# Window attention, MLP and an inverted bottleneck on one core: depthwise matrices placed by the host and scaled on GpSimd, the attention bias looked up by rows, x loaded per group

## The chip, the core and the metric
One core of a Trainium2 chip. The metric is the device time of one execution in microseconds (us). TensorE (PE), VectorE (DVE), ScalarE (ACT), GpSimd (POOL) and SyncE (SP, which here only issues DMAs) each run a program of their own in order and meet at semaphores. All data are float32.

## What is computed
x is (4, 48, 128, 128). The first layer is a Swin block without shift, the second an inverted residual with batch norms:

```python
h = layernorm(x) cut into 8x8 windows of 64 tokens, 48 channels, 4 heads of 12
attn = softmax(q @ k.T * scale + rpb_table[rel_idx])       # bias (64, 64) a head, the same in every window
x = x + proj(attn @ v)
x = x + fc2(gelu(fc1(layernorm(x))))                       # 48 -> 192 -> 48
h = relu(bn1(w1 @ x))                                      # 48 -> 288
h = relu(bnd(depthwise3x3(h, wd)))                         # 288 channels
out = x + bn2(w2 @ h)                                      # 288 -> 48
```

## The kernel before
Three stages follow each other, each a pipeline written out by hand with a loop in its middle.

**Attention** (`attention`, from L232) works on 128 groups of 4 pairs of windows, 512 tokens each. Step i of every engine handles different stages of groups i-3 to i+4. DVE sums and centres group i+4 (L509, L528), GpSimd squares and scales (L624, L615), TensorE turns it and makes queries and keys of group i+2 (L449, L469), ACT copies the keys out (L595), and SyncE moves them by four DMAs into `kb`, the right operand of the scores (L410). The first 64 rows of `kb` hold the bias, the first 64 rows of `qa` an identity, so the score product L441 adds the bias itself. All of x lies in one tile `scratch`. ACT loads its first groups (L356), SyncE the rest in three DMAs (L400), in its program ahead of the keys' DMAs.

Before the first step, `prepare_tables` (L81) does two things in the same tile `scratch`. It looks the bias up: the indices of all 4096 pairs are spread to 128 partitions, cast, compared with the partition's number (L161, L164), and the one-hot matrix is multiplied with the table, 512 columns at a time (L211); the result, 4 x 4096, goes to DRAM and from there, spread, into `kb` (L137, L143). And it builds the depthwise matrices: a 3x3 filter over a patch of 10x10 inputs and 8x8 outputs is a matrix of 100 rows and 64 columns for each of 288 channels. 192 products of the scaled taps with a tensor of places (L222) make them, DVE and ACT copy them out (L185, L201), and SyncE stores them to `conv_mats` in DRAM, nine parts of 32 channels (L148). Row 100 of each carries the batch norm's shift. The x loads of L400 wait for these stores.

**MLP** (`mlp`, L630) works on 64 strips, 5.8 us each, and writes the image rows to `img_mid` in DRAM.

**Convolution** (`conv`, L805) has its GpSimd program written before that of `mlp`, and those of SyncE, TensorE, ACT and DVE behind it; each engine runs its programs in the order in which they are written. There are 8 half images and 3 chunks of 96 channels in each, so k = 0 to 23. A half image is cut on GpSimd into patches `xp`: 16 pieces, each two DMAs into one of five slots and a copy (L930). The first half is loaded by GpSimd itself, piece by piece (L985), as soon as its image is stored; later ones by SyncE (L1020). Its GpSimd order at the start is: constants (L964), weight loads (L973), the clearing of `yc` (L974, L976), the 16 pieces, the borders. DVE folds the batch norms into the weights (L1172 to L1191) after its MLP program. Chunk k on TensorE is the depthwise stage (L1084, three thirds with a tile `mats` each), then the products of w2 (L1118) mixed with the first products of chunk k+1 (L1066). SyncE asks for the next matrices third by third as the depthwise stage lets go of them (L1028), in the first chunk of a half followed by the pieces of the next half. TensorE's first product waits for the cut of the first half (`border_set`) and for the weights.

Of the kernel before, what the change touches and what calls it, by code (L numbers as in the profile page):

```python
# [28 lines left out]
P = 128  # L29
# [29 lines left out]
TAPROW = 32  # L59
# [21 lines left out]
def prepare_tables(nc, d, block, scratch, psum, kb, kb_set):  # L81


# [7 lines left out]
    taps = sb("taps", [P, HID1])  # L91
    gd, vd, md, bd = (sb(n, [TAPROW + 1, HID1]) for n in ("gd", "vd", "md", "bd"))
    sd, shift = sb("sd", [TAPROW + 1, HID1]), sb("shift", [TAPROW + 1, HID1])
    eps = sb("eps_d", [P, 1])


    size = [POUT * P, CH * POUT]
    scratch = scratch[:, scratch.shape[1] - size[0] - 2 * size[1]:]
    places = scratch[:, 0:size[0]].rearrange("q (o i) -> q o i", o=POUT)
    onehot = scratch[:, size[0]:size[0] + 2 * NT * NT].rearrange("q (t n) -> q t n", t=2)  # L100
    idsf = scratch[:, size[0] + 2 * NT * NT:size[0] + 3 * NT * NT]
    bias = idsf[0:NH, :]
    mats = [scratch[:, size[0] + size[1] * k:size[0] + size[1] * (k + 1)].rearrange("q (c o) -> q c o", o=POUT)
            for k in range(2)]
    cleared, loaded, ids_loaded, cast = sem("t_cleared"), sem("t_loaded"), sem("ids_loaded"), sem("ids_cast")
    hot, looked_up, copied, stored, kb_loaded = (
        sem(n) for n in ("hot", "looked_up", "b_copied", "b_stored", "kb_loaded"))
    bn_loaded, table_loaded = sem("bn_loaded"), sem("table_loaded")
    root, scaled = sem("d_root"), sem("d_scaled")
    mat_ready, copied_v, copied_a = sem("mat_ready"), sem("mat_cv"), sem("mat_ca")  # L110
    mats_stored = [sem(f"mat_stored{k}") for k in range(2)]
    K = TAPROW + 1
    UNIT = 4
    NU = POUT // UNIT
    BLOCKS = NT * NT // 512

    @block.gpsimd
    def _(pool):
        for n, (t, value) in enumerate(((eps[:, :], EPS), (table[:, :, :], 0.0), (taps[:, :], 0.0),
                                       (places, 0.0))):  # L120
            nc.gpsimd.memset(t, value).then_inc(cleared, 1)
            pool.wait_ge(cleared, n + 1)

    @block.sync
    def _(sp):
        for dst, src in ((ids[:, :], d["rel_idx"].partition_broadcast(P)), (number[:, :], d["number"])):
            sp.dma_start(dst, src).then_inc(ids_loaded, 16)
        for t, n in ((vd, "vd"), (gd, "gd"), (md, "md"), (bd, "bd")):
            sp.dma_start(t[:, :], d[n].partition_broadcast(K)).then_inc(bn_loaded, 16)
        sp.wait_ge(cleared, 2)  # L130
        for t, rows in ((0, slice(0, P)), (1, slice(P, d["table"].shape[0]))):
            sp.dma_start(table[0:rows.stop - rows.start, t, :], d["table"][rows, :]).then_inc(table_loaded, 16)
        sp.wait_ge(cleared, 4)
        sp.dma_start(taps[0:9, :], d["wd"]).then_inc(loaded, 16)
        sp.dma_start(places[0:K, :, :], d["places"]).then_inc(loaded, 16)
        sp.wait_ge(copied, BLOCKS)
        sp.dma_start(d["rel_bias"], bias).then_inc(stored, 16)  # L137
        sp.wait_ge(stored, 16)
        sp.wait_ge(*kb_set)
        for s in range(2):  # L140
            for h in range(NH):
                src = d["rel_bias"][h].rearrange("(n m) -> n m", m=NT)
                sp.dma_start(kb[s][0:NT, :, h, :], bc(src, 1, 2 * PAIRS)).then_inc(kb_loaded, 16)  # L143
        for c in range(CHUNKS):
            sp.wait_ge(copied_v, NU // 2 * (c + 1))
            sp.wait_ge(copied_a, NU // 2 * (c + 1))
            for u in range(LOADS):
                sp.dma_start(d["conv_mats"][LOADS * c + u], mats[c % 2][0:MROWS, TCH * u:TCH * u + TCH, :])\  # L148
                    .then_inc(mats_stored[c % 2], 16)

    def mats_free(eng, c):

        if c == 1:
            eng.wait_ge(stored, 16)
        if c >= 2:
            eng.wait_ge(mats_stored[c % 2], 16 * LOADS * (c // 2))

    @block.vector
    def _(dve):
# [3 lines left out]
        for t in range(2):  # L163
            nc.vector.tensor_scalar(onehot[:, t, :], idsf, number[:, t:t + 1], None, ALU.is_equal).then_inc(hot, 1)  # L164
        dve.wait_ge(root, 1)
        nc.vector.reciprocal(vd[:, :], sd[:, :]).then_inc(scaled, 1)
        dve.wait_ge(scaled, 1)
        nc.vector.tensor_tensor(sd[:, :], vd[:, :], gd[:, :], ALU.mult).then_inc(scaled, 1)
        dve.wait_ge(scaled, 2)
        nc.vector.tensor_tensor(md[:, :], md[:, :], sd[:, :], ALU.mult).then_inc(scaled, 1)  # L170
        dve.wait_ge(loaded, 32)
        nc.vector.tensor_tensor(taps[0:9, :], taps[0:9, :], sd[0:9, :], ALU.mult).then_inc(scaled, 1)
        dve.wait_ge(scaled, 4)
        nc.vector.tensor_tensor(shift[:, :], bd[:, :], md[:, :], ALU.subtract).then_inc(scaled, 1)
        dve.wait_ge(scaled, 5)
        nc.vector.tensor_copy(taps[TAPROW:K, :], shift[0:1, :]).then_inc(scaled, 1)
        for j in range(0, BLOCKS, 2):
            dve.wait_ge(looked_up, j + 1)
            nc.vector.tensor_copy(bias[:, 512 * j:512 * j + 512], psum[0:NH, j, :]).then_inc(copied, 1)
        for c in range(CHUNKS):  # L180
            mats_free(dve, c)
            for u in range(NU * c, NU * (c + 1), 2):
                dve.wait_ge(mat_ready, u + 1)
                j = UNIT * (u % NU)
                nc.vector.tensor_copy(mats[c % 2][0:MROWS, :, j:j + UNIT].rearrange("q c o -> q o c"),  # L185
                                      psum[0:MROWS, u % 8, 0:UNIT * CH].rearrange("q (o c) -> q o c", c=CH)).then_inc(copied_v, 1)

    @block.scalar
    def _(act):
        act.wait_ge(bn_loaded, 64)  # L190
        act.wait_ge(cleared, 1)
        nc.scalar.activation(sd[:, :], vd[:, :], ACT.Sqrt, bias=eps[0:K, :]).then_inc(root, 1)
        for j in range(1, BLOCKS, 2):
            act.wait_ge(looked_up, j + 1)
            nc.scalar.activation(bias[:, 512 * j:512 * j + 512], psum[0:NH, j, :], ACT.Copy).then_inc(copied, 1)
        for c in range(CHUNKS):
            mats_free(act, c)
            for u in range(NU * c + 1, NU * (c + 1), 2):
                act.wait_ge(mat_ready, u + 1)
                j = UNIT * (u % NU)  # L200
# [5 lines left out]
    def _(pe):  # L206
# [10 lines left out]
        for u in range(CHUNKS * NU):  # L217
            if u >= 8:
                pe.wait_ge(copied_a if u % 2 else copied_v, (u - 8) // 2 + 1)
# [1087 lines left out]
```

## Time and profile before

| what | value |
|---|---|
| median of 3 runs | 2379.42 us (2370.36 to 2392.66) |
| the profiled execution, its own time | 2378.27 us |
| its span | 2376.5 us |
| PE busy | 2216.1 us (93%) |
| PEld (weight loads, beside PE) | 1575.1 us (66%) |
| DVE busy | 1560.4 us (66%) |
| ACT busy | 1392.0 us (59%) |
| POOL busy | 408.3 us (17%) |
| mean granted TensorE clock | 0.975 |

The span runs from the first to the last instruction of the profile. "Idle before" in a row is the time its engine stood still ahead of it, and the arrow names what ended that. A float32 product appears as two records of TensorE. SPq, ACTq and the DMA lines of POOL are the issuing of DMAs, not their transfers.

### The profile page before, as it was taken

How to read it: one execution, taken by the hardware profiler on the slowest of the kernel's cores; microseconds unless marked ns; L12 is line 12 of the kernel's file. 1: busy time of each engine (PE TensorE's matmuls, PEld its weight loads, DVE VectorE, ACT ScalarE, POOL GpSimd, SP SyncE). 2: the span in 40 equal slices, each digit the busy share in tenths (PEclk: the TensorE clock that was granted, in tenths of full speed). 3: DMA queues.
4: the chain of work that ended last, by engine and by line, in shares of the span. 5: the costliest groups of instructions: out<-in, count | busy, mean ns of one | idle time of the engine just before them, and what ended most of it. 6: DMA issues, size and time to landing. Idle time of an engine off the chain costs nothing.

```text
span 2376.5 us, 71361 instructions
## 1 busy us (share of the span) xinstructions
PE 2216.1 (93%) x27044; PEld 1575.1 (66%) x27044; DVE 1560.4 (66%) x2869; ACT 1392.0 (59%) x2896; POOL 408.3 (17%) x796
## 2 busy tenths in 40 slices
PE   5499999999999995999999899999999999989997
PEld 3477777777777774333333577767777776767774
DVE  5279999999999896333333566657565666656663
ACT  1367777777777773555555455556556565555653
POOL 2023333333333334513000010101010101001000
PEclk9799999999999997999999999999999999999999
DMA  3811111111111111545444433526172535343411
GB/s 121 310 41 51 54 51 54 51 54 51 54 51 54 51 55 56 129 119 139 117 113 114 112 79 91 114 68 138 49 149 56 113 93 106 89 99 69 117 52 28
DMA packets 272936, 208.57 MB, mean 88 GB/s; under 512 B 228011, under 2 KB 261401, under 8 KB 262217
## 3 DMA queue, kind: packets, MB, share of 16 engines
q1 hardware_dynamic: 269992, 200.62, 32.3%
q0 software_dynamic: 1728, 2.93, 0.7%
q8 instruction: 142, 2.33, 0.4%
q10 hardware_dynamic: 1014, 2.21, 0.3%
q14 instruction: 60, 0.49, 0.1%
HBM read 130.05 MB, written 63.05 MB: 81 GB/s over the span
## 4 chain that ended last, share of the span: by engine, by line
PE 53%; ACT 4%; issue 2%; DVE 1%; SPq 0%; DMA 0%; ACTq 0%; DVEq 0%
PE psum L1084 11%; PE psum L1066 11%; PE psum L1118 10%; PE psum L1126 5%; PE psum L740 5%; PE psum L733 5%; PE psum L726 3%; PE psum L744 3%; ACT h2T L1157 3%; ACT h L906 1%; ACT room L906 0%; SPq L693 0%; DVE room L767 0%; ACT room L799 0%; DVE room L1172 0%
## 5 line engine op out<-in xcount | busy, mean ns | idle before, releaser
L1066 PE MATMUL psum<-ew,xp 64*100 64x96 f32 x6144 | 355.7, 256 | 37.4 <-ACT h L906 13.5
L1157 ACT ACTIVATE h2T<-psum 96x512 f32<-96x512 f32 x384 | 227.1, 591 | 208.0 <-PE psum L1126 207.8
L907 DVE TENSOR_SCALAR h<-psum 100x384 f32<-100x384 f32 x384 | 211.9, 557 | 207.9 <-PE psum L1066 207.1
L1066 PEld LDWEIGHTS psum<-ew,xp 64*100 64x100 f32 x6144 | 310.3, 168 | 50.3 <-issue 16.8
L1118 PE MATMUL psum<-h2T,pw 128*64 128x256 f32 x1536 | 308.2, 406 | 9.4
L441 PE MATMUL psum<-kb,qa 128*64 128x256 f32 x2048 | 251.9, 388 | 29.9 <-DMA kb<-kk 29.9
L1084 PE MATMUL psum<-h,mats 128*64 128x128 f32 x4608 | 270.2, 275 | 6.7 <-issue 5.7
L1084 PEld LDWEIGHTS psum<-h,mats 128*64 128x64 f32 x4608 | 263.5, 138 | 11.6 <-issue 7.8
L906 ACT ACTIVATE room<-psum 64x512 f32<-64x512 f32 x288 | 169.8, 590 | 150.7 <-PE psum L1084 147.2
L907 DVE TENSOR_SCALAR room<-psum 64x512 f32<-64x512 f32 x288 | 199.9, 694 | 82.5 <-PE psum L1084 78.1
L906 ACT ACTIVATE h<-psum 100x384 f32<-100x384 f32 x384 | 186.1, 491 | 100.3 <-PE psum L1066 67.0
L930 POOL COPY xp<-piece 128x400 f32<-128x400 f32 x128 | 67.5, 527 | 1004.4 <-DMA piece<-img_mid 1002.7
L799 ACT ACTIVATE room<-psum,room 128x512 f32<-128x512 f32 x192 | 131.9, 688 | 153.2 <-PE psum L740 132.4
L525 DVE TENSOR_REDUCE top<-psum 128x16 f32<-128x1024 f32 x128 | 156.7, 1224 | 72.1 <-PE psum L441 72.1
L1126 PEld LDWEIGHTS psum<-ident,room 64*96 64x96 f32 x3072 | 113.8, 124 | 135.9 <-issue 133.2
L441 PEld LDWEIGHTS psum<-kb,qa 128*64 128x64 f32 x2048 | 136.9, 138 | 98.6 <-issue 32.0
L775 DVE TENSOR_TENSOR room<-psum,room 128x512 f32<-128x512 f32 x64 | 44.3, 692 | 224.8 <-PE psum L733 207.4
L1126 PE MATMUL psum<-ident,room 64*96 64x64 f32 x3072 | 165.9, 227 | 4.8 <-issue 2.5
L569 ACT ACTIVATE vb<-psum 64x96 f32<-64x96 f32 x512 | 128.0, 250 | 53.0 <-PE psum L493 48.3
L573 ACT ACTIVATE xnT<-psum 128x256 f32<-128x256 f32 x128 | 49.1, 383 | 186.3 <-PE psum L449 186.3
L1118 PEld LDWEIGHTS psum<-h2T,pw 128*64 128x64 f32 x1536 | 103.2, 135 | 80.6 <-ACT h2T L1157 47.6
L532 DVE TENSOR_TENSOR prob<-psum,top 128x1024 f32<-128x1024 f32 x128 | 155.8, 1217 | 0.1
(154 smaller groups left out, 3587.4 us busy)
## 6 DMA issues: line engine op xcount, KB each, us to landing
mats<-conv_mats SPq DMA_DIRECT2D x72, 896.0 KB, 6.1
tok_mid<-mid SPq DMA_DIRECT2D x128, 224.0 KB, 1.9
room<-tok_mid SPq DMA_DIRECT2D x64, 448.0 KB, 3.4
piece<-img_mid SPq DMA_DIRECT2D x196, 63.8 KB, 2.4
img_mid<-room SPq DMA_DIRECT2D x128, 97.5 KB, 2.6
kb<-kk SPq DMA_DIRECT2D x512, 24.0 KB
out<-yc SPq DMA_DIRECT2D x16, 768.0 KB, 8.1
conv_mats<-scratch SPq DMA_DIRECT2D x9, 896.0 KB, 7.2
```

What stands on the lines that cost most here:

```text
L441: mm = nc.tensor.matmul(ps_s[NT * w:NT * w + NT, p // 2, 256 * (p % 2):256 * (p % 2) + 256], qa[s][:, NT * n:NT * n + NT], kb[s][:, n, :, ...
L525: nc.vector.tensor_reduce(top[s][:, :], sc, AX_X, ALU.max).then_inc(top_done, 1)
L532: nc.vector.tensor_tensor(prob[s][:, :, :], sc, bc(top[s][:, :], 2, NT), ALU.subtract)\
L569: last = nc.scalar.activation(dst, v[NT * w:NT * w + NT, :, h, :], ACT.Copy)
L799: nc.scalar.activation(hid[s][:, k, :], ps_h[:, k, :], ACT.Gelu, bias=(b1r if k == 2 else b1)[:, 0:1]).then_inc(gelu_done, 1)
L906: return nc.scalar.activation(dst, src, ACT.Relu)
L907: return nc.vector.tensor_scalar(dst, src, 0.0, None, ALU.max)
L1066: mm = nc.tensor.matmul(ring[(j + u) % 4][0:PIN, p:4 * CH:4], xp[hx][rows, 2 * j + p, :], w1[rows, c, :], start=True, stop=True)
L1084: mm = nc.tensor.matmul(bank[:, n % 4:4 * PATCHES:4], mats[ch // TCH][:, ch % TCH, :], h1[:, ch, :], start=True, stop=True)
L1118: mm = nc.tensor.matmul(ps_y[n % 2][64 * r:64 * r + 64, 0:POUT * STEPS[n - 2][2]], w2[:, c, :], h2T[n % 2][:, r, :], start=True, stop=True)
L1126: mm = nc.tensor.transpose(ps_t[0:CH, r, POUT * p:POUT * p + POUT], h2[rows, PR * pc + a + p, :], ident[rows, rows])
L1157: nc.scalar.activation(h2T[n % 2][0:CH, :, :], ps_t[0:CH, :, 0:POUT * PART], ACT.Copy).then_inc(copied, 1)
```

## The change
The host now lays each channel's nine taps out in a matrix (`placed_taps`, with ones in row 100), and this input `taps` is what the convolution loads. The scale of the depthwise batch norm, with its shift in row 100, is one tile `scale`, and GpSimd multiplies each loaded part of 32 channels by its columns in place (`scale_mats`); TensorE waits for `mats_scaled` instead of `mats_loaded`. For chunk 0 GpSimd loads and scales the matrices itself, between its weight loads and the clearing of `yc`. The four vectors of the depthwise batch norm are loaded into the last `mats` tile (`dn`), and ACT and DVE prepare them beside the other norms. GpSimd's cuts of a half now follow the scaling of that half's second chunk.

The bias is looked up with the one-hot matrix as the weights: 64 pairs of products, one for each key position, each giving 64 query rows and 4 heads, in PSUM in the layout that `kb` has. DVE and ACT copy it into both `kb` tiles (`put_bias`), half each. `prepare_tables` is replaced by `find_bias`, whose programs are written ahead of attention's other ones.

x is loaded group by group: two by ACT, each further one by SyncE, two steps before DVE sums it, behind that step's four key DMAs.

```diff
-def prepare_tables(nc, d, block, scratch, psum, kb, kb_set):
+def find_bias(nc, d, block, scratch, psum):
     @block.gpsimd
     def _(pool):
-        for n, (t, value) in enumerate(((eps[:, :], EPS), (table[:, :, :], 0.0), (taps[:, :], 0.0),
-                                       (places, 0.0))):
+        nc.gpsimd.memset(table[:, :, :], 0.0).then_inc(cleared, 1)
...
     @block.tensor
     def _(pe):
         pe.wait_ge(table_loaded, 32)
         pe.wait_ge(hot, 2)
-        for j in range(BLOCKS):
+        for m in range(NT):
+            half, at = divmod(m, NT // 2)
             for t in range(2):
-                mm = nc.tensor.matmul(psum[0:NH, j, :], table[:, t, :], onehot[:, t, 512 * j:512 * j + 512],
+                mm = nc.tensor.matmul(psum[0:NT, half, at:NH * NT // 2:NT // 2], onehot[:, t, m, :], table[:, t, :], start=(t == 0), stop=(t == 1))
-        for u in range(CHUNKS * NU):
...
+        def put_bias(eng, write, half):
+            eng.wait_ge(looked_up, 1)
+            eng.wait_ge(fixed, FIXED)
+            cols = slice(NT // 2 * half, NT // 2 * half + NT // 2)
+            found = psum[0:NT, half, 0:NH * NT // 2].rearrange("q (h m) -> q h m", h=NH)
+            for s in range(2):
+                write(kb[s][0:NT, :, :, cols], bc(found, 1, 2 * PAIRS)).then_inc(bias_put, 1)
...
# attention, SyncE's step
+                if has(i + 6):
+                    sp.wait_ge(sum_done, i + 5)
+                    load_x(sp, i + 6, s)
# attention, DVE's step
-                    if isinstance(i, int):
-                        x_here(dve, i + 4 if i < 5 else GROUPS - 1)
+                    dve.wait_ge(x_loaded[s], x_loads(i + 4, s))
...
# conv, GpSimd
+        def scale_mats(pool, k):
+            for s in range(LOADS):
+                pool.wait_ge(*((mats_loaded[s], 16 * k) if k else (mats_begun[s], 16)))
+                at = CH * (k % CHUNKS) + TCH * s
+                m = mats[s][0:MROWS, :, :]
+                nc.gpsimd.tensor_tensor(m, m, bc(scale[0:MROWS, at:at + TCH], 2, POUT), ALU.mult).then_inc(mats_scaled, 1)
+                pool.wait_ge(mats_scaled, LOADS * k + s + 1)
...
             for dst, src in loads:
                 pool.dma_start(dst, src).then_inc(w_loaded, 16)
+            for s in range(LOADS - 1):
+                pool.dma_start(mats[s][0:MROWS, :, :], d["taps"][s]).then_inc(mats_begun[s], 16)
+            pool.wait_ge(w_ready, 4)
+            pool.dma_start(scale[PIN:PIN + 1, :], dn["b"][0:1, :]).then_inc(shift_put, 16)
+            pool.wait_ge(shift_put, 16)
+            pool.dma_start(mats[-1][0:MROWS, :, :], d["taps"][LOADS - 1]).then_inc(mats_begun[-1], 16)
+            scale_mats(pool, 0)
             nc.gpsimd.memset(y[:, 0:H // 2, :], 0.0).then_inc(y_done, 1)
...
-            for h in range(1, HALVES):
-                pool.wait_ge(unit_ready, ready_before_depthwise(CHUNKS * (h - 1)))
+            pool.wait_ge(border_set, 2)
+            for k in range(1, HALVES * CHUNKS):
+                scale_mats(pool, k)
+                h = k // CHUNKS + 1
+                if k % CHUNKS != 1 or h == HALVES:
+                    continue
                 for j in range(PR):
...
# conv, TensorE
-                        pe.wait_ge(mats_loaded[d // (DEPTHS // LOADS)], 16 * (k + 1))
+                        pe.wait_ge(mats_scaled, LOADS * k + d // (DEPTHS // LOADS) + 1)
```

## Rows read from the trace of the kernel before
**Rows 1.** Groups by line, 0 to 150 us: busy us, mean ns | idle before, releaser
```profile
L222 PE MATMUL psum<-taps,scratch 128*112 128x96 f32 x384 | 38.0, 262 | 0.8 <-ACT scratch L195 0.8
...
L441 PE MATMUL psum<-kb,qa 128*64 128x256 f32 x80 | 12.4, 464 | 29.9 <-DMA kb<-kk 29.9
```
**Rows 2.** Timeline, 76 to 125 us: start us, us, engine, line, operation
```profile
82.30 1.28 ACT L555 ACT_TABLE_LOAD   x1
...
87.16 0.59 ACT L595 ACTIVATE kk<-psum 48x512 f32<-48x512 f32 x1 [0.82 <-PE psum L469]
...
92.36 1.30 SPq L297 DMA_DIRECT2D scratch<-in_x_tokens  x3
...
120.41 3.68 PE L441 MATMUL psum<-kb,qa 128*64 128x256 f32 x16 [29.90 <-DMA kb<-kk]
```
**Rows 3.** Timeline, one step of attention's loop, 300 to 309 us
```profile
300.92 1.12 PE L487 MATMUL psum<-vb,probT 128*64 128x26 f32 x32
...
301.64 3.31 SPq L410 DMA_DIRECT2D kb<-kk  x4
...
302.59 1.95 PE L441 MATMUL psum<-kb,qa 128*64 128x256 f32 x16
...
308.83 1.95 PE L441 MATMUL psum<-kb,qa 128*64 128x256 f32 x16
```
**Rows 4.** Timeline, the seam from the MLP to the convolution
```profile
1327.17 1.94 DVE L1172 RECIPROCAL room<-room 128x288 f32<-128x288 f32 x1
...
1331.30 0.46 DVE L1186 TENSOR_TENSOR room<-room 128x288 f32<-128x288 f32 x1
...
1332.96 15.48 PE L1066 MATMUL psum<-ew,xp 64*100 64x96 f32 x256 [6.50 <-DVE ew L1191]
```
**Rows 5.** Line L985, the piece loads that GpSimd issues itself
```profile
L985 POOL DMA_DIRECT2D piece<-img_mid x32: 656/657/722, 1053.0 to 1123.1; - x32
...
DMA to landing us min/median/max: 2.6/3.2/4.5
```
**Rows 6.** Timeline, 0 to 28 us
```profile
0.76 0.42 SPq L127 DMA_DIRECT2D ids<-in_rel_idx  x1
...
12.63 6.93 POOL L121 MEMSET scratch<- 128x8192 f32 x1
12.64 6.95 DVE L374 TENSOR_SCALAR w_qk<-qkv_w,ln_g 48x48 f32<-48x48 f32 x1
...
20.21 2.27 DVE L161 CAST scratch<-ids 128x4096 f32<-128x4096 int32 x1
20.32 0.61 ACTq L360 DMA_DIRECT2D w_qk<-qk_row  x1
...
22.52 4.62 DVE L164 TENSOR_SCALAR scratch<-scratch,number 128x4096 f32<-128x4096 f32 x2
```
**Rows 7.** DMA issues: line, engine, count, KB each, median us to landing
```profile
mats<-conv_mats SPq DMA_DIRECT2D x72, 896.0 KB, 6.1
...
ids<-in_rel_idx SPq DMA_DIRECT2D x1, 2048.0 KB, 7.4
...
kb<-rel_bias SPq DMA_DIRECT2D x8, 128.0 KB, 2.7
```
**Rows 8.** Groups by line on GpSimd, whole span
```profile
L930 POOL COPY xp<-piece 128x400 f32<-128x400 f32 x128 | 67.5, 527 | 1004.4 <-DMA piece<-img_mid 1002.7
...
L624 POOL TENSOR_TENSOR sq<-cen 128x192 f32<-128x192 f32 x128 | 64.8, 506 | 62.6 <-DVE cen L528 62.6
...
L974 POOL MEMSET yc<- 128x2048 f32 x1 | 1.8, 1815 | 0.0
```
**Rows 9.** Timelines of SyncE's queue and of TensorE, first and second chunk
```profile
1353.21 7.46 SPq L1028 DMA_DIRECT2D mats<-conv_mats  x3
1361.00 25.31 SPq L1020 DMA_DIRECT2D piece<-img_mid  x32
1394.29 48.53 SPq L1028 DMA_DIRECT2D mats<-conv_mats  x6
...
1390.46 10.94 PE L1084 MATMUL psum<-h,mats 128*64 128x128 f32 x190
```

More of the change, by code:

```diff
@@ L90, in prepare_tables @@
     table, number = sb("table", [P, 2, NH]), sb("number", [P, 2])
[L91 to L115, printed above, removed]
+    scratch = scratch[:, scratch.shape[1] - 3 * NT * NT:]
+    onehot = scratch[:, 0:2 * NT * NT].rearrange("q (t m n) -> q t m n", t=2, n=NT)
+    idsf = scratch[:, 2 * NT * NT:3 * NT * NT]
+    cleared, ids_loaded, table_loaded, cast, hot, looked_up = (
+        sem(n) for n in ("t_cleared", "ids_loaded", "table_loaded", "ids_cast", "hot", "looked_up"))
     @block.gpsimd
     def _(pool):
-        for n, (t, value) in enumerate(((eps[:, :], EPS), (table[:, :, :], 0.0), (taps[:, :], 0.0),
-                                       (places, 0.0))):
-            nc.gpsimd.memset(t, value).then_inc(cleared, 1)
-            pool.wait_ge(cleared, n + 1)
+        nc.gpsimd.memset(table[:, :, :], 0.0).then_inc(cleared, 1)
     @block.sync
@@ L127, in _ @@
             sp.dma_start(dst, src).then_inc(ids_loaded, 16)
-        for t, n in ((vd, "vd"), (gd, "gd"), (md, "md"), (bd, "bd")):
-            sp.dma_start(t[:, :], d[n].partition_broadcast(K)).then_inc(bn_loaded, 16)
-        sp.wait_ge(cleared, 2)
+        sp.wait_ge(cleared, 1)
         for t, rows in ((0, slice(0, P)), (1, slice(P, d["table"].shape[0]))):
             sp.dma_start(table[0:rows.stop - rows.start, t, :], d["table"][rows, :]).then_inc(table_loaded, 16)
[L133 to L156, printed above, removed]
     @block.vector
@@ L163, in _ @@
         for t in range(2):
[L164 to L200, printed above, removed]
-                nc.scalar.activation(mats[c % 2][0:MROWS, :, j:j + UNIT].rearrange("q c o -> q o c"),
-                                     psum[0:MROWS, u % 8, 0:UNIT * CH].rearrange("q (o c) -> q o c", c=CH), ACT.Copy)\
-                    .then_inc(copied_a, 1)
@@ L354, in _ @@
                 act.dma_start(dst, src).then_inc(w_loaded, 16)
-            for part in range(2):
-                load_x(act, part)
+            for g in range(2):
+                load_x(act, g, g)
             act.wait_ge(row_put, 2)
@@ L1137, in _ @@
             nc.scalar.activation(c2["t"][:, :], c2["v"][:, :], ACT.Sqrt, bias=eps[:, :]).then_inc(root, 1)
+            nc.scalar.activation(dn["t"], dn["v"], ACT.Sqrt, bias=eps[0:MROWS, :]).then_inc(root, 1)
             def expanded(k, which):
@@ L1253, in block_program, with placed_taps @@
     conv(nc, d)
-def tap_places():
-    places = np.zeros((TAPROW + 1, POUT, P), np.float32)
+def placed_taps(wd):
+    taps = wd.reshape(HID1 // TCH, TCH, 9)
+    placed = np.zeros((HID1 // TCH, MROWS, TCH, POUT), np.float32)
     for r in range(PH):
```

89 lines of the change are left out of this document (38 added, 51 removed).

## Prediction
> **What bounds the kernel now.** I read the page's slices first: TensorE is busy in nearly all of them, and dark in three places, the first slices, the seam between attention and MLP, and the seam between MLP and convolution. In the first 150 us the groups by line show the removed matmuls (L222, 38.0 us) and, at L441, 29.9 us of idle TensorE that a DMA of keys ended [rows 1]. The timeline says why: the preparation of the depthwise matrices lasts until about 82 us, SyncE then issues three big loads of x at 92.36 and the keys' DMAs only behind them, and the first score matmul starts at 120.41 although its keys left ACT at 87.75 [rows 2]. From there to about 905 us one group of attention takes 308.83 - 302.59 = 6.24 us, with no wait on TensorE [rows 3]. At the third seam TensorE starts the convolution at 1332.96, some 6.5 us after the MLP's last matmul [rows 4], with the first half image already cut (that ran on GpSimd beside the MLP, 1053 to 1124 us [rows 5]). A chunk of the convolution then takes 41 us, filled by TensorE, with GpSimd nearly idle.
>
> So three stages change: the start (until 120.41), the seam before the convolution (until 1332.96), and what runs in the loops.
>
> **The start: removed 120.4 us, added 45.3.** Gone are L222 with its copies, its nine stores, the round trip of the bias and the wait of the keys behind 10 MB of x. What is left is one chain. The indices' DMA, issued at 0.76, lands 7.4 us later, the numbers 0.5 us after it [rows 6, 7]: 8.7. The cast (2.27) and two compares (4.62) [rows 6]: 15.6. The look-up is now 128 products, each a load of 64 columns of weights and 4 columns moved, 256 records. The nearest row is L487, 32 records of the same weights with 26 columns in 1.12 us, 35 ns each [rows 3]: 9.0 us at full clock. At half clock all of it would be 1.9 times that, by L441 at 3.68 cold [rows 2] against 1.95 warm [rows 3]: 17 us. TensorE comes from idle, so its first part is slow; I take 11.5: 27.1. Behind it, in TensorE's order now, stands the product for the bias row, and behind that three one-row operations of DVE: 1.3 us, my estimate from instructions of 0.2 to 0.6 us: 28.4. ACT issues four DMAs of 0.61 [rows 6]: 30.9. Then its two bias copies, 1024 elements a partition from PSUM; by L595, 512 elements in 0.59 [rows 2], 2.4 us, with a table load of 1.28 before and one behind (today's start has two as well; one is in [rows 2]): 35.9. DVE does its two copies earlier. From the end of ACT's table load (83.58) to the keys in SBUF (87.75) it is 4.2 us today [rows 2]: 40.1. Four key DMAs, the last issued 2.5 us on (four take 3.31 [rows 3]) and landed 2.7 later [rows 7]: first score matmul at **45.3**, 75.1 us earlier. Bounds: the look-up 9.0 to 17; no table loads, -2.6; the weights' bias rows landing after 7.4 rather than 2.7 us, +0.6. So 40 to 52, a gain of 68 to 80. The ramp behind it is the same cold one.
>
> GpSimd's constants (done at about 12 us now) now run beside the cast and the compares. Today one long memset of 6.93 us holds three tiny DVE operations for 6.95 us [rows 6]. The memsets left are 0.5 us or less by then, so DVE loses at most about 1 us; if they wait for DVE instead they end by 19, still ahead of 27. The Trainium skill's SBUF — State Buffer (Who interferes with whom) has the rule: whichever of the two engines takes the shared port pair first keeps it for its whole instruction, and the other blocks fully. The trace agrees (6.95 beside 6.93). The same page speaks against the change further on, since GpSimd now reads SBUF for 300 us of the convolution; but it says that a DVE instruction with at most one SBUF input outside the 2-port modes does not contend, and there DVE's inputs are PSUM or PSUM with one SBUF operand, so by the rule the sum is unchanged.
>
> **Attention's loop: 0.** SyncE gets one load of 96 KB a step, some 0.4 us, behind 3.31 us of key issues [rows 3] and one store: about 4.1 of 6.24. It is issued two steps (12 us) before DVE's new wait, and lands in 2 to 3 us. Queued behind that wait on DVE is the whole step, but TensorE waits for nobody there, and DVE is busy about 90% of the time. If the wait's register work cost 0.1 us and nothing hid it, it would be 12 us over 122 steps. I take 0; bounds 0 and 12.
>
> **The seam before the convolution: added 89 us.** This is the dear part. GpSimd's program for the convolution now stops at a wait for DVE's fourth step of weight preparation, and DVE and ACT reach that only when their MLP programs are through. Behind that wait on GpSimd are the first scaling, the clearing of y and all 16 cuts of the first half image, which today run during the MLP. In order:
> - DVE's fourth step ends at about 1331.8 today. The four tiles dn add a reciprocal of 1.94 and three products of 0.46 [rows 4], back to back about 3.0, and ACT's extra root at most 0.1: 1334.9.
> - One row by DMA: between 2.6 and 3.2 us to land by GpSimd's own loads [rows 5]: 1337.8. The issue of the last taps, 0.66: 1338.5. They land in 6.1 [rows 7], under the scaling of the other two.
> - Three scalings of 112x2048. No row has this size. 128x192 takes 0.506 [rows 8]. All proportional, 5.4 each; if about 0.1 of it is fixed, 4.4. I take 4.4, since every GpSimd operation here starts with a like fixed part: with two short waits 1351.8. The Trainium skill's GPSIMD Engine Reference (3.1 Elementwise) gives 4497 ns for such a product of 2048 elements; by that the sum would be 0.3 us more.
> - Two memsets of y, 1.81 each [rows 8], with their waits 3.8: 1355.6.
> - Sixteen pieces one after another, each two issues, a landing and a copy. Today 15 periods take 1123.1 - 0.7 - 1053.0 = 69.4, 4.63 each, beside the MLP's traffic [rows 5]. The floor is 0.66 + 2.6 + 0.53 and a little: 3.9 [rows 5, 8]. The traffic is gone, so I take 4.1: 65.6, until 1421.2. Borders 1.0: TensorE starts at **1422.2** instead of 1332.96.
> Delay 89.2; bounds 84 (pieces at 3.9) and 101 (4.63, scalings at 5.4).
>
> **The convolution's loop: 0.** Today the three matrix DMAs of a chunk are issued from 1353.21 to 1360.7 and the next depthwise stage starts at 1390.46 [rows 9]. With 6.1 us to land the first arrives at 1359.3; three scalings are done by 1372.5 (5.4 each: 1375.5), 15 us or more ahead. In the first chunk of a half the 16 cuts now queue behind them. SyncE's loads of pieces wait for the cuts (25.31 us for 32 DMAs [rows 9]), so SyncE leaves this about 7 to 10 us later, near 1395, when the next matrix request is due (1394.3). The matrices of that chunk are then scaled by about 1418, wanted at 1431. Covered; the cover ends when a scaling takes some 8 to 10 us.
>
> **Sum**, against the profiled execution's own 2378.3 (1.1 below the median of the runs shown): 2378.3 - 75.1 + 89.2 = **2392.4**, +0.6%. Own range 2382 to 2414. A measurement of this kernel can tell from no change about 1%, that is outside 2356 to 2403.
>
> **The rivals.**
> - *GpSimd's serial pieces stay slow (slower than before).* The place is the seam, the price 16 us for each us of piece period, and it decides above 4.76 us a piece (16 x 0.66 = 10.6 over my sum gives 2403). At 5.0: 2407. For it: 4.63 today, landings up to 4.5 [rows 5]. Against it: the MLP's transfers, beside which these were measured, are over. Chance 0.12.
> - *The attention step grows.* DVE's wait or SyncE's extra load shows in each of 122 steps; 0.1 us gives 2405, decides at 0.09. For it: DVE is the second busiest engine there. Against it: DVE idles about 0.6 us a step. Chance 0.07.
> - *The scaling surfaces in the loop.* At 12 us an operation the second chunk of each half would come some 10 us late, seven times: 2462. It needs 8 to 10 us against my 4.4 to 5.4. Chance 0.05.
> - *The seam does not move.* If the first matrices could be scaled and the half cut beside the MLP as today, only the gain at the start would stay: 2303. The order of the programs on DVE and ACT speaks against it. With it, in the same direction, pieces much quicker than the floor: at 3.0 us 2375, not yet 1% faster. Together 0.06.
> - My forecast, with all of its own bounds inside: 0.70.
>
> **The numbers.** Slower by over 1%: 0.24, the first three. Faster: 0.06. Same: 0.70. The range of 2374 to 2416 takes in the forecast's own bounds, the first rival up to 5.3 us a piece and half of the second.
>
> **What would show it.** Right: L441 first at 40 to 52; the look-up 9 to 17 us; an idle TensorE of 90 to 100 us before the first L1066, its chain being GpSimd's piece loads and copies; scalings at 4.4 to 5.4 us; attention steps of 6.24 and chunks of 41 us. Wrong: a first L441 after 55 or an idle seam under 80 or over 110; a matmul L1084 waiting for GpSimd inside the loop.

## Result and profile after

The changed kernel takes 2398.86 us (median of 20 runs, 2387.80 to 2415.49), the kernel before 2378.57 us (20 runs, 2365.73 to 2392.66). The ratio is 1.0086, with a 95% interval of 1.0061 to 1.0111: 0.9% slower, inside the 1% that I had set as "no change", though the interval reaches a little past it. The profiled execution took 2392.04 us, with a span of 2390.2 us and a mean granted clock of 0.969; it lies in the lower half of its runs.

The total came out near the forecast, but several terms did not. I cut both spans at three instructions that both kernels have: the first score matmul (L341 now, L441 before), DVE's first reciprocal of the convolution's weights (L1097, before L1172), and the first product of the convolution (L990, before L1066).

| stretch | before | after | difference |
|---|---|---|---|
| start to first score matmul | 120.41 | 61.25 | -59.2 |
| to the first reciprocal (attention, MLP) | 1206.76 | 1214.06 | +7.3 |
| to the convolution's first product (seam) | 5.79 | 87.35 | +81.6 |
| to the end | 1043.5 | 1027.5 | -16.0 |
| span | 2376.5 | 2390.2 | +13.7 |

The start, on the timeline of the changed kernel (start us, us, engine, line, operation); it stands against [rows 1, 2, 6]:

```profile
8.71 2.83 POOL L245 MEMSET xn<- 128x256 f32 x2
8.99 2.29 DVE L109 CAST scratch<-ids 128x4096 f32<-128x4096 int32 x1 [8.99 <-DMA number<-in_number]
11.32 4.75 DVE L112 TENSOR_SCALAR scratch<-scratch,number 128x4096 f32<-128x4096 f32 x2
...
16.22 27.44 PE L122 MATMUL psum<-table,scratch 128*64 128x4 f32 x256 [16.22 <-DVE scratch L112]
...
44.90 0.61 ACTq L263 DMA_DIRECT2D w_qk<-qk_row  x1
...
47.51 1.28 ACT L265 ACT_TABLE_LOAD   x1 [47.51 <-issue]
...
48.80 1.93 ACT L265 ACTIVATE kb<-psum 64x1024 f32<-64x1024 f32 x2
...
50.74 1.28 ACT L454 ACT_TABLE_LOAD   x1
...
56.30 3.47 SPq L307 DMA_DIRECT2D kb<-kk  x4
...
61.25 1.12 PE L341 MATMUL psum<-kb,qa 128*64 128x256 f32 x4 [2.21 <-DMA kb<-kk]
```

One row stands out: L122, the look-up, 256 records in 27.44 us, 107 ns each. TensorE waits 2.21 us for keys where it waited 29.90 [rows 2].

The seam, on the same timeline; it answers to [rows 4, 5]:

```profile
1277.51 1.93 DVE L1097 RECIPROCAL mats<-dscale 112x288 f32<-112x288 f32 x1
...
1282.48 0.45 DVE L1111 TENSOR_TENSOR mats<-mats 112x288 f32<-112x288 f32 x1
...
1283.22 0.50 POOL L891 DMA_DIRECT2D dscale<-mats  x1 [360.44 <-DVE mats L1111]
1285.06 0.54 POOL L893 DMA_DIRECT2D mats<-in_taps  x1 [1.34 <-DMA dscale<-mats]
1285.66 11.00 POOL L860 TENSOR_TENSOR mats<-mats,dscale 112x2048 f32<-112x2048 f32 x3
1296.72 1.81 POOL L895 MEMSET yc<- 128x2048 f32 x1
1298.65 1.81 POOL L897 MEMSET yc<- 128x2048 f32 x1
1300.75 1.41 POOL L906 DMA_DIRECT2D piece<-img_mid  x2 [0.29 <-POOL yc L897]
...
1357.90 1.34 POOL L906 DMA_DIRECT2D piece<-img_mid  x2
...
1362.66 7.54 PE L990 MATMUL psum<-ew,xp 64*100 64x96 f32 x114 [88.08 <-POOL xp L851]
```

GpSimd had waited 360.44 us at `w_ready`. After that come the row by DMA, the scalings, the clearing of y and the 16 pieces, one after another, and TensorE stands still for 88.08 us.

The first half of the MLP, for which the forecast had no term, on the same timeline:

```profile
921.74 1.04 POOL L889 DMA_DIRECT2D mats<-in_taps  x2
...
921.94 0.42 SPq L597 DMA_DIRECT2D room<-tok_mid  x1
...
923.56 1.99 PE L639 MATMUL psum<-room 128*128 128x512 f32 x4
925.47 1.08 PE L643 MATMUL psum<-room 128*64 128x512 f32 x4
926.48 1.08 PE L625 MATMUL psum<-room 128*112 128x128 f32 x8
...
929.37 1.99 PE L639 MATMUL psum<-room 128*128 128x512 f32 x4
...
938.73 1.96 PE L625 MATMUL psum<-room 128*112 128x128 f32 x8 [6.36 <-DMA room<-tok_mid]
...
943.65 0.30 PEld L639 LDWEIGHTS psum<-room 128*128 128x128 f32 x2 [1.04 <-issue]
```

Two loads of taps (896 KB each) go out at 921.74. The strip of 448 KB that SyncE asks for at 921.94, two steps before its use, lands after 16.7 us and keeps TensorE waiting until 938.73. The step from L639 to L639 takes 14.28 us instead of 5.81 (929.37 less 923.56, the step before), 8.5 us more: 6.36 are the wait, and the other 2.1 are products at a granted clock of 0.50 behind it (L625 takes 1.96 us instead of 1.08).

The convolution's loop: groups of TensorE by line (busy us, mean ns, idle before, what ended it), from the first full chunk on, of the changed kernel

```profile
L990 PE MATMUL psum<-ew,xp 64*100 64x96 f32 x5888 | 334.8, 252 | 19.7 <-ACT h L810 14.1 <-ACT h2T L1082 5.5
...
L1008 PE MATMUL psum<-h,mats 128*64 128x128 f32 x4603 | 272.5, 277 | 6.0 <-issue 6.0
```

and of the kernel before:

```profile
L1066 PE MATMUL psum<-ew,xp 64*100 64x96 f32 x5888 | 340.2, 255 | 30.9 <-ACT h L906 13.5 <-issue 12.2 <-ACT h2T L1157 5.1
...
L1084 PE MATMUL psum<-h,mats 128*64 128x128 f32 x4608 | 270.2, 275 | 6.7 <-issue 5.7 <-DVE h L907 1.0
```

12.2 us of "issue", time in which TensorE waited for nothing that the profile shows, are gone from the expansion product, and the same 5888 products are 5.4 us less busy. No part of the change was meant to do that. TensorE never waits for `mats_scaled` after the seam; from the page:

```profile
L860 POOL TENSOR_TENSOR mats<-mats,dscale 112x2048 f32<-112x2048 f32 x72 | 260.7, 3621 | 563.1 <-DMA mats<-in_taps 560.0
```

### The profile page after: what moved, and what is told of

Same layout as the page of the kernel before. It is cut to its first block, busy times and chain, and to the rows that moved or that the text cites. A ratio compares the mean times of both kernels' runs of the same rounds, so it can differ in the third digit from the quotient of the medians.

```text
span 2390.2 us, 71604 instructions
## 1 busy us (share of the span) xinstructions
PE 2186.2 (91%) x26884; PEld 1558.5 (65%) x26884; DVE 1534.1 (64%) x2841; ACT 1371.1 (57%) x2870; POOL 672.1 (28%) x873
## 4 chain that ended last, share of the span: by engine, by line
PE 52%; ACT 4%; DMA 3%; issue 2%; POOL 1%; DVE 1%; SPq 0%; ACTq 0%; DVEq 0%; POOLq 0%
PE psum L1008 11%; PE psum L990 10%; PE psum L1042 10%; PE psum L1050 5%; PE psum L639 5%; PE psum L632 5%; PE psum L625 3%; ACT h2T L1082 3%; PE psum L643 3%; DMA piece<-img_mid 2%; ACT h L810 1%; DMA room<-tok_mid 1%; ACT room L810 1%; POOL mats L860 0%; POOL piece L906 0%
## 5 line engine op out<-in xcount | busy, mean ns | idle before, releaser
L990 PE MATMUL psum<-ew,xp 64*100 64x96 f32 x6144 | 349.5, 253 | 108.0 <-POOL xp L851 88.1
L860 POOL TENSOR_TENSOR mats<-mats,dscale 112x2048 f32<-112x2048 f32 x72 | 260.7, 3621 | 563.1 <-DMA mats<-in_taps 560.0
L990 PEld LDWEIGHTS psum<-ew,xp 64*100 64x100 f32 x6144 | 304.6, 165 | 120.7 <-issue 92.9
L341 PE MATMUL psum<-kb,qa 128*64 128x256 f32 x2048 | 251.0, 387 | 2.6 <-DMA kb<-kk 2.2
L341 PEld LDWEIGHTS psum<-kb,qa 128*64 128x64 f32 x2048 | 136.7, 137 | 70.6 <-issue 3.9
L514 POOL TENSOR_TENSOR xn<-cen,rstd 128x192 f32<-128x192 f32 x128 | 64.8, 506 | 336.3 <-ACT rstd L484 336.3
```

What stands on the lines that cost most here:

```text
L341: mm = nc.tensor.matmul(ps_s[NT * w:NT * w + NT, p // 2, 256 * (p % 2):256 * (p % 2) + 256], qa[s][:, NT * n:NT * n + NT], kb[s][:, n, :, ...
L860: nc.gpsimd.tensor_tensor(m, m, bc(scale[0:MROWS, at:at + TCH], 2, POUT), ALU.mult).then_inc(mats_scaled, 1)
L990: mm = nc.tensor.matmul(ring[(j + u) % 4][0:PIN, p:4 * CH:4], xp[hx][rows, 2 * j + p, :], w1[rows, c, :], start=True, stop=True)
```

## Experiments

Medians stand against the kernel before, run on the same chip (2376.99 for the first group of runs, 2380.16 for the second, 2380.08 for the third).

### The start alone

The start of the change, the convolution of before, loading taps that nothing scales: the scale and the shift of the depthwise norm are left out.

```diff
-            pool.wait_ge(w_ready, 4)
-            pool.dma_start(scale[PIN:PIN + 1, :], dn["b"][0:1, :]).then_inc(shift_put, 16)
...
-            scale_mats(pool, 0)
-                        pe.wait_ge(mats_scaled, LOADS * k + d // (DEPTHS // LOADS) + 1)
+                        pe.wait_ge(mats_loaded[d // (DEPTHS // LOADS)], 16 * (k + 1))
```

> The changed attention part (row look-up, x by groups, no preparation) with the convolution of before, whose matrices SyncE loads as host-placed taps without any scaling: the scale and shift of the depthwise norm are left out. Theory (the start gives 59.2 us, 120.4 to 61.2, and nothing in the loops pays for it): 2378.6 - 59 = 2319 us. Rival (x by groups or fewer stores change the loops as well): off by more than 8 us from that.

Measured: 2311.36 us (2298.78 to 2326.42), ratio 0.9743 (0.9671 to 0.9816). The timeline of its start shows the look-up unchanged and the first score matmul 59.3 us earlier than before:

```profile
16.10 27.44 PE L122 MATMUL psum<-table,scratch 128*64 128x4 f32 x256 [16.10 <-DVE scratch L112]
...
61.14 3.68 PE L341 MATMUL psum<-kb,qa 128*64 128x256 f32 x16 [2.22 <-DMA kb<-kk]
```

So the start is worth about 59 us. The median is some 6 us better than the start explains, 7.6 below the 2319 expected, so only just inside the 8 that the rival asked for; with four runs from 2299 to 2326 the median can't settle that. The profile says more: its span is 79.5 us shorter than before (2297.0), of which the start is 59.3 and the stretch from the first expansion product on 20.4 (1023.1 against 1043.5). Here too the expansion product has no "issue" waits.

### The convolution alone

The convolution of the change behind the start of before, which still builds and stores `conv_mats`, though nothing loads them any more.

```diff
+            pool.wait_ge(w_ready, 4)
+            pool.dma_start(scale[PIN:PIN + 1, :], dn["b"][0:1, :]).then_inc(shift_put, 16)
...
+            scale_mats(pool, 0)
-                        sp.dma_start(mats[s][0:MROWS, :, :], d["conv_mats"][LOADS * ((c + 1) % CHUNKS) + s])\
+                        sp.dma_start(mats[s][0:MROWS, :, :], d["taps"][LOADS * ((c + 1) % CHUNKS) + s])\
```

> The kernel before with the convolution part of the change alone; the preparation still runs and its matrices are not used. Theory (the convolution part costs the seam's 81.5 us and the MLP's stall of 8.5, and its loop nothing): 2378.6 + 90 = 2469 us. Rival (the 16 us that the changed kernel's convolution loop was shorter in its profile, 959.5 against 975.9 from first to last depthwise stage, belong to the change): 2453 us.

Measured: 2466.41 us (2460.11 to 2471.28), ratio 1.0366 (1.0313 to 1.0418), 89.4 us slower: the seam's 81.6 and the MLP step's 8.5 make 90.1. (The 8.5 are the changed kernel's; in this profile the slowest strip lands after 14.7 us and TensorE waits 4.4 us for it, so the size of this stall differs from run to run.) Its expansion product, all of the span:

```profile
L1091 PE MATMUL psum<-ew,xp 64*100 64x96 f32 x6144 | 356.5, 256 | 121.2 <-POOL xp L952 88.1 <-issue 14.7 <-ACT h L911 13.5
```

The same 88.1 of idle at the seam, but 14.7 us of "issue" are still there. So the convolution's part of the change doesn't remove these waits. The two medians add up: -65.6 + 89.4 = +23.8, against +20.3 for the whole change.

### x group by group alone

```diff
-            for part in range(2, len(X_PARTS) - 1):
-                load_x(sp, part)
...
+                if has(i + 6):
+                    sp.wait_ge(sum_done, i + 5)
+                    load_x(sp, i + 6, s)
```

> The kernel before with x loaded group by group and nothing else changed; SyncE no longer has three big loads ahead of the keys. Theory (the keys' wait was for the queue behind 10 MB of x): the first score matmul starts near 93 us instead of 120.4, as soon as the preparation is over, so 2378.6 - 27 = 2351 us. Rival (the preparation's nine stores hold the keys up by themselves): the first score matmul stays after 110 us and the gain is under 10 us.

Measured: 2358.68 us (10 runs, 2352.38 to 2369.92), ratio 0.9920 (0.9897 to 0.9943), 18.3 us faster. I had expected more. Its timeline, SyncE and TensorE:

```profile
92.85 0.84 SPq L296 DMA_DIRECT2D scratch<-in_x_tokens  x2
96.84 0.69 PE L448 MATMUL psum<-ident,xn 128*128 128x128 f32 x2 [9.64 <-POOL xn L613]
96.85 3.47 SPq L406 DMA_DIRECT2D kb<-kk  x4
...
101.83 2.79 PE L440 MATMUL psum<-kb,qa 128*64 128x256 f32 x11 [1.53 <-DMA kb<-kk]
```

The wait for keys falls from 29.9 to 1.5 us, but the next groups of x are also asked for only at 92.85, behind the wait for the matrices' stores, and a 9.64 us wait for the scaled x takes its place. Taken alone this part moves the first score by 18.6 of the 59 us; the other 40.6 need the look-up and the missing matrix preparation.

### The cuts ahead of the wait

```diff
-            pool.wait_ge(w_ready, 4)
...
-            scale_mats(pool, 0)
             nc.gpsimd.memset(y[:, 0:H // 2, :], 0.0).then_inc(y_done, 1)
...
             close_borders(pool, 0, 0)
             pool.wait_ge(border_set, 2)
+            pool.wait_ge(w_ready, 4)
...
+            scale_mats(pool, 0)
```

> The changed kernel with one reordering on GpSimd: the clearing of y and the 16 pieces come before the wait for DVE's fourth step, the scaling of the first matrices behind it. Theory (the serial pieces behind that wait are the cost of the seam): the pieces run beside the MLP again, TensorE's first L990 starts about 9 us after the MLP's last DVE instruction instead of 87, so 78 us earlier, and the scaling (2 us of DMA, then 11 us) hides under the first chunk's 15.5 us of expansion: about 2321 us against 2399. Rival (the scaling itself is the cost): the first depthwise products then wait for the scaled matrices, and 15 to 20 us of the 78 come back: about 2338. Either way the 8.5 us stall of the MLP beside the first taps loads stays.

Measured: 2323.74 us (2309.47 to 2331.63), ratio 0.9785 (0.9730 to 0.9841). Its expansion product from 1270 us on:

```profile
L990 PE MATMUL psum<-ew,xp 64*100 64x96 f32 x6144 | 350.0, 253 | 30.9 <-ACT h L810 14.1 <-DVE ew L1116 9.5 <-ACT h2T L1082 5.5
```

TensorE waits 9.5 us at the seam, for DVE (6.5 before [rows 4]; the 3.0 more are DVE's work on `dn`), and in no row for a scaling, though the first three now come after the cuts. So the seam's price is the place of the cuts, not the scalings. The median is 3 us from the theory's number and 14 from the rival's; its interval reaches to both, so the verdict rests on this row.

### The taps' loads later

```diff
+            pool.wait_ge(w_ready, 4)
             for s in range(LOADS - 1):
                 pool.dma_start(mats[s][0:MROWS, :, :], d["taps"][s]).then_inc(mats_begun[s], 16)
-            pool.wait_ge(w_ready, 4)
```

> The changed kernel with the first two taps loads issued by GpSimd behind its wait for DVE instead of ahead of it. Theory (their 1.8 MB hold up one strip load of the MLP, which landed after 16.7 us instead of 3.3): every strip load lands within 6 us, no MLP step is longer than 6.2 us (one of 14.3 now), 8.5 us go; the seam grows by about 5 us, since the first scaling waits for its taps (6 to 9 us) instead of starting at once. Rival (the other weight loads of GpSimd are the cause): the long MLP step stays.

Measured: 2392.45 us, the changed kernel's own time (2392.04 profiled). The landing of the MLP's strips (the L597 source view) has no such outlier (6.9 is the longest, where I had expected 6), where the changed kernel has a maximum of 16.7:

```profile
DMA to landing us min/median/max: 3.1/3.3/6.9
```

TensorE waits for no strip, and the stretch from the first score to DVE's first reciprocal is 6.1 us shorter (1208.0 against 1214.06). But the timeline of the seam shows where that gain went:

```profile
1277.55 1.05 POOL L890 DMA_DIRECT2D mats<-in_taps  x2 [354.32 <-DVE mats L1111]
1278.59 0.50 POOL L891 DMA_DIRECT2D dscale<-mats  x1
1287.72 0.54 POOL L893 DMA_DIRECT2D mats<-in_taps  x1 [8.63 <-DMA dscale<-mats]
...
1365.65 4.65 PE L990 MATMUL psum<-ew,xp 64*100 64x96 f32 x52 [96.74 <-POOL xp L851]
```

The one row, issued behind the two big loads, lands after 9.1 us instead of 1.8, and TensorE waits 96.74 instead of 88.08: 8.7 us, where I had expected about 5. The cause of the MLP's stall is shown (it leaves with the loads); this edit only moved the time into the seam.

### Why the look-up takes 107 ns a record

Two products kept apart instead of added up in PSUM (rows of the table from 128 on are left out of the sum), and the output written in one piece instead of with a stride:

```diff
-                mm = nc.tensor.matmul(psum[0:NT, half, at:NH * NT // 2:NT // 2], onehot[:, t, m, :], table[:, t, :], start=(t == 0), stop=(t == 1))
+                mm = nc.tensor.matmul(psum[0:NT, half + 2 * t, at:NH * NT // 2:NT // 2], onehot[:, t, m, :], table[:, t, :], start=True, stop=True)
```

> The changed kernel with the second product of each pair written to a bank of its own and not added: the rows of the table from 128 on are left out of the bias. Theory A (the 107 ns a record come from the accumulation onto the product before): the 256 records take 9 to 14 us instead of 27.4. Theory B (TensorE's clock stays at its lower level) and theory C (the strided output): unchanged, 27.4.

```diff
-                mm = nc.tensor.matmul(psum[0:NT, half, at:NH * NT // 2:NT // 2], ...
+                mm = nc.tensor.matmul(psum[0:NT, half, NH * at:NH * at + NH], ...
```

> The changed kernel with the look-up's four results next to each other in PSUM instead of 32 columns apart; the copies read them strided. Theory C (the strided output costs): 9 to 14 us for the 256 records instead of 27.4. Theories A (accumulation) and B (clock): unchanged, and the copies take the same 1.2 and 1.0 us within a few tenths.

Measured: 2388.05 and 2391.47 us, and in the timeline of either the look-up lasts the same 27.44 us. Neither accumulating nor the stride counts. The row of the kernel with two banks:

```profile
16.60 27.44 PE L122 MATMUL psum<-table,scratch 128*64 128x4 f32 x256 [16.60 <-DVE scratch L112]
```

Then TensorE was kept busy ahead of the look-up (80 more products of zeros):

```diff
+        pe.wait_ge(warm_set, 1)
+        for n in range(80):
+            nc.tensor.matmul(psum[0:NT, 2, 0:64], warm[:, 0:NT], warm[:, 0:64], start=True, stop=True)
         pe.wait_ge(table_loaded, 32)
```

> The changed kernel with 80 products (160 records) of a zero tile on TensorE ahead of the look-up, while TensorE would wait for DVE. Two questions. First, the look-up: theory B (the 256 records run at the lower clock level) gives 13 to 16 us if the clock, once up, stays up through them, and 27.4 again, after a faster first part, if they cannot keep it up; theories A and C give 27.4. Second, the convolution: the changed kernel has 160 records fewer of TensorE than the one before, and waits marked issue on L990 of 12 to 15 us in sum are gone from it. If these depend on where the code of the loop lies, the 160 records bring back waits of over 4 us at L990; if they depend on the data transfers of the preparation, they stay away.

Measured: 2410.49 us. Its timeline, and two stretches of it (the columns are busy us and records of PE, PEld, DVE, ACT, POOL, then the granted clock):

```profile
1.00 11.54 PE L122 MATMUL psum<-warm 128*64 128x64 f32 x160 [1.00 <-POOL warm L99]
15.83 27.44 PE L128 MATMUL psum<-table,scratch 128*64 128x4 f32 x256 [3.28 <-DVE scratch L115]
```

```profile
4.00:12.00 8.00, 8.00 (x129) 8.00 (x128) 3.57 (x2) 0.00 (x0) 7.69 (x6) 1.00 0.59 194
...
20.00:24.00 4.00, 4.00 (x40) 4.00 (x40) 0.00 (x0) 0.00 (x0) 0.00 (x0) 0.50 0.02 4
```

From 4 to 12 us the warm products run at 62 ns a record with a granted clock of 1.00 (2.4 GHz). Then TensorE idles 3.28 us, and the look-up runs under a granted clock of 0.50 (1.2 GHz), again in 27.44 us. The column falls at about 15.7, before the look-up's first record. When the same kernel ran again (below), it fell at about 16.6, 0.4 us behind the look-up's first record, and the look-up took 27.07 us, 0.37 less. The changed kernel's own clock column shows 1.00 in this stretch, but its pace is the same to the last digit, so the look-up there ran at the lower level too.

Last, one product of zeros with 512 columns before every four products of the look-up, behind 160 warm ones:

```diff
+            if m % 2 == 0:
+                nc.tensor.matmul(psum[0:NT, 2, 0:512], warm[:, 0:NT], wide[:, 0:512], start=True, stop=True)
```

> The changed kernel with 160 zero products ahead of the look-up and one product of 512 columns in front of every second pair of the look-up (32 of them, 64 records). Theory B (the look-up's 27.4 us are its records at the lower clock level, and so few columns cannot keep the level up): the wide products keep the granted clock at full, a wide record takes 0.21 us and a look-up record 35 to 60 ns, 23 to 29 us in all. Rival (the records of the look-up take 107 ns at any clock): 13.7 + 27.4 = 41 us at full clock, or 55 if the clock stays low.

Measured: 2425.40 us. Its timeline in one period, 39.55 to 40.87, and its weight loads by line:

```profile
39.55 1.05 PE L129 MATMUL psum<-wide,warm 128*64 128x512 f32 x2
...
40.44 0.58 PE L131 MATMUL psum<-table,scratch 128*64 128x4 f32 x8
...
40.87 1.05 PE L129 MATMUL psum<-wide,warm 128*64 128x512 f32 x2
```

```profile
L131 PEld LDWEIGHTS psum<-table,scratch 128*64 128x64 f32 x256 | 20.0, 138 | 18.7 <-issue 18.7
```

A period has 2 wide records and 8 of the look-up; from the first of these (40.44) to the next wide one (40.87) are 0.43 us, 54 ns a record, at a granted clock of 1.00. Their weight loads take 138 ns, against 227 in the changed kernel. I had priced a wide record at half its 0.44 us, so the whole stretch (22.35 to 64.8, some 42.5 us) missed my number and comes near the rival's 41; the record's own price is what tells them apart, and it is the faster one. So the look-up ran at 107 ns because TensorE was at the lower level, and at the higher one it costs 54 to 55.

### "Issue" waits that come and go

The kernel with 80 warm products, timed:

> The kernel of e8 again, timed: 160 records of TensorE more at the start, in time in which it would wait, and nothing else. Theory (the place of the code costs the loop its waits): 8 to 18 us above the changed kernel's 2398.9, so 2407 to 2417. Rival (the one run of e8 was chance): within 5 us of 2399.

Measured: 2410.29 us (2399.20 to 2415.45), ratio 1.0116 (1.0055 to 1.0178); the profiled span is 2408.7, as in the run above, 18.5 above the changed kernel's. Its start is unchanged (the products lie in idle time). Its convolution, from 1270 us on:

```profile
L996 PE MATMUL psum<-ew,xp 64*100 64x96 f32 x6144 | 355.8, 256 | 116.1 <-POOL xp L857 89.2 <-ACT h L816 13.5 <-issue 8.3
...
L1014 PE MATMUL psum<-h,mats 128*64 128x128 f32 x4608 | 268.9, 275 | 9.7 <-issue 8.8 <-DVE h L817 0.8
```

The waits are back (8.3 us here, 10.6 in the run above) and so are the 6 us of busy time (355.8 against 349.5), from 160 records of TensorE more, a thousand us earlier, and nothing changed in the convolution. Over all kernels: before 12.2, x alone 14.6, the convolution alone 14.7, the wide products between 8.5 (384 records more); the other seven profiles (the change, the start alone, the cuts first, the late taps, the two look-ups with another output, all mends together) have 0.5 at most. What the two groups differ in is how many instructions stand ahead of the loop in TensorE's program (the first three still make the tables). From the first expansion product to the end, the six profiles with these waits take 1037.9 to 1048.4 us and the seven without 1022.7 to 1027.8. The spans show it too (2386 to 2391 us in four kernels without these waits, 2408.7 twice with them); the timed ratios overlap (1.0061 to 1.0111 and 1.0055 to 1.0178), so its price is settled only as far as these profiles go. That it is the place of the code is not shown: the padded kernel also has one more tile, memset and semaphore, and no run changes one of these alone.

### All mends together

The cuts first, the taps' loads behind them and behind `w_ready`, the bias row's product ahead of the look-up, and one table load instead of two on ACT's way:

```diff
+            pe.wait_ge(w_loaded, 16 * W_LOADS)
+            nc.tensor.matmul(ps_a[0:1, 0:3 * C], ln_b[:, :], qkv_w[0:C, :], start=True, stop=True).then_inc(w_bias, 1)
         bias_ctx, looked_up = find_bias(nc, d, block, scratch, psum)
...
+            nc.scalar.preload_act_table_set("natural_log_exp_and_others")
             put_bias(act, lambda dst, src: nc.scalar.activation(dst, src, ACT.Copy), 1)
...
             close_borders(pool, 0, 0)
             pool.wait_ge(border_set, 2)
+            pool.wait_ge(w_ready, 4)
+            for s in range(LOADS - 1):
+                pool.dma_start(mats[s][0:MROWS, :, :], d["taps"][s]).then_inc(mats_begun[s], 16)
...
+            scale_mats(pool, 0)
```

> Four things together, all of the computation kept: the pieces before GpSimd's wait (as in e1), the first taps loads behind it (as in e4), TensorE's product for the bias row ahead of the look-up so that ACT's row DMAs run beside it, and ACT's table loaded once at the start instead of twice around the bias copies. Theory (the terms add up): 2323.7 - 8.5 (stall of the MLP) - 3.9 (the bias row and the DMA issues off the path) - 2.6 (table loads) = 2309 us; first score matmul near 55 us instead of 61.2; the scaling still under the first chunk's expansion. Rival (the late taps loads reach the first depthwise products): TensorE waits 3 to 8 us for the scaled matrices, 2312 to 2317.

Measured: 2300.96 us (6 runs, 2299.65 to 2313.91), ratio 0.9681 (0.9635 to 0.9726): 3.2% faster than the kernel before, where the changed kernel is 0.9% slower. Its timeline:

```profile
57.14 3.68 PE L341 MATMUL psum<-kb,qa 128*64 128x256 f32 x16 [2.22 <-DMA kb<-kk]
...
1271.51 8.72 PE L988 MATMUL psum<-ew,xp 64*100 64x96 f32 x121 [9.48 <-DVE ew L1114]
```

The start is 63.3 us shorter than before, the seam costs 3.0, and no row has TensorE waiting for a strip or a scaling. The first score comes at 57.14 where I had expected 55: behind its copies ACT waits 2.28 us for DVE's sums, so not all of the saved table loads is gained. The total is 8 us below the 2309 expected, and no run explains this; the 2323.7 that it was reckoned from is a median of four runs between 2309 and 2332.

## Why the prediction was right, and where it was not

The total was right within 7 us, and that was luck: errors offset each other. Against the forecast of +14.1 us in the profiled execution stands +13.7, made of other terms. One of the forecast's own signs of being wrong came true, a first score after 55 us (it came at 61.25); the idle seam, 88.08, lies a little under the 90 to 100 named as right and not under the 80 named as wrong.

- **The start, -75.1 forecast, -59.2 measured, outside the bounds of 68 to 80.** The step that failed is the look-up, 11.5 us with bounds 9 to 17, where 27.44 was measured; the 15.9 us between are the whole error. I took 35 ns a record from L487 [rows 3], and 1.9 times that as the end of the range. Both parts were low: at the higher clock level the record costs 54 to 55 ns (256 of them 14), and at the lower one, at which it ran, 107. L487 was also not the same kind of product. By the code, its products write PSUM partitions 0 to 63 and 64 to 127 by turns, and those of the look-up always 0 to 63. Rows at a granted clock of 1.00 bear the difference out: of 512 columns, a record of L643, which goes by turns too, takes 0.25 us (four from 925.47 to 926.48), one of L639, which writes all 128 partitions, 0.48, and a wide one on 0 to 63 alone 0.44. No run changes this by itself. Every other term was within 1 us: numbers landed at 8.99 (8.7), compares done at 16.07 (15.6 forecast), 1.2 us to ACT's first DMA (1.3), ACT's two copies and two table loads 4.6 (5.0), then 4.3 to the keys in SBUF (4.2) and 5.0 to the first score (5.2).
- **GpSimd's constants beside DVE: right.** Its memsets of `xn`, `on` and `sq` waited for DVE: two of 128x256 took 2.83 us, where two of 128x512 had taken 1.11 before the cast began, and all were done at 18.0, by the 19 I had given. DVE lost at most 0.15 us (2.29 and 4.75 against 2.27 and 4.62). The Trainium skill's SBUF — State Buffer (Who interferes with whom) says of a DVE instruction in a 2-port mode that the engine that comes first keeps the shared ports for its instruction; these rows agree. Its other sentence, that DVE with one SBUF input or fewer, outside these modes, doesn't contend, agrees too: DVE's copy out of PSUM in the convolution takes 557 ns in both kernels, with and without 260.7 us of scaling on GpSimd beside it.
- **Attention's loop, 0: right.** Its step is 6.25 us, against 6.24 [rows 3]. The rival of a growing step fell.
- **The seam, +89.2 forecast, +81.6 measured, mechanism as told, below the lower bound of 84.** DVE's extra work was 3.0 (3.0). The row by DMA took 1.84 (2.9), a scaling 3.62 (4.4), a piece 3.81 (1357.90 less 1300.75 over 15; I took 4.1 and called 3.9 the floor). These give 1.1, 2.3 and 4.6 us back. The bound of 84 didn't come out of its own condition: pieces at 3.9 take 3.2 off 89.2, to 86.0. The top of the forecast's own range, 2414, is 2411 by its bounds (2378.3 - 68 + 101). The GPSIMD Engine Reference of the Trainium skill (3.1 Elementwise) has 4497 ns for an addition of two float32 tensors of 2048 elements; here, with 112 partitions and a second operand broadcast along 64 columns, 3621 were measured, and the measurement decides. The rival of slow pieces fell; the one of a seam that doesn't move fell too, for the kernel as it stands, but the reordered kernel shows what it was worth.
- **The convolution's loop, 0 for scaling: right**, but the stretch got 16.0 us shorter, of which the forecast had nothing: the "issue" waits.
- **Missed altogether: the taps' loads in the MLP, +8.5.** I had counted SyncE's and GpSimd's new DMAs at the seam and in the loops, but the two loads that stand ahead of GpSimd's wait start 360 us before it.

The sum of the errors: +15.9 (look-up) - 7.6 (seam) + 8.5 (MLP step) - 16.0 (issue waits) - 1.2 (attention and MLP otherwise) = -0.4, and 14.1 less 0.4 are the 13.7 of the spans. That the forecast of the total held says little for its terms.

## What to carry to other kernels

When a wait is put into an engine's program, look at both sides of it: everything behind it moves to its release (here 16 cuts that had been hidden, 61 us), and everything that could be issued ahead of it still starts early, in a stage that has no room for it. Order by what the late event is really needed for; with the cuts ahead of the wait the same change is 2.1% faster than before instead of 0.9% slower, and with all mends 3.2%. Price many small products from a record of the same kind, down to the part of PSUM that it writes, at the clock level that the stage will have, not from a busy stage.

## What the hardware showed that I had not expected

- A float32 record with 4 columns takes 54 to 55 ns at the higher clock level and 107 at the lower, hardly less than one with 64 columns (62 at the higher). L487's records with 26 columns take 35 [rows 3]; they write the two halves of the PSUM partitions by turns, which is the likely reason, but not tested.
- Neither adding up in PSUM nor a strided output changed the look-up by 0.01 us.
- 3.28 us of idle TensorE behind 11.54 us of products, the last 8 at 62 ns a record, were followed by a look-up at a granted clock of 0.50 throughout, although its records followed each other without a gap. In one run the clock had fallen before the look-up began, in the other 0.4 us into it.
- The clock column can miss a low level: it shows 1.00 over the changed kernel's look-up, which runs exactly as slow as the one under 0.50.
- A start with 160 more records of TensorE changed its "issue" waits in a loop more than 1300 us later from none to 8.3 and 10.6 us, with 6 us more busy time.
- A strip of 448 KB that usually lands in 3.3 us took 16.7 beside two loads of 896 KB (14.7 and 16.0 in two other kernels with these loads), and a DMA of one row behind them 9.1 instead of 1.8.
